# Attention scores made a second time transposed, with the maxima as extra rows, and values multiplied in float32 by four heads

## The chip, the cores and the metric

One core of one Trainium2 chip runs the whole program. The metric is device time in microseconds (us) of one execution, the median of several. The engines are TensorE (PE: matmuls and transposes; PEld is its weight load), VectorE (DVE), ScalarE (ACT), GpSimd (POOL) and SyncE (SP, which here only issues DMAs). Every engine runs its own program in order and waits on semaphores.

## The reference, cut to what matters

Two layers of an adaptive-layernorm model on X of 4 x 512 tokens x 256. Layer 0 is causal attention with 16 heads of 16, then a mixture of experts; layer 1 is a gated convolution, an MLP and another mixture of experts. The change is in layer 0's attention:

```
Q, K, V = heads(Xn @ Wq + bq), heads(Xn @ Wk + bk), heads(Xn @ Wv + bv)
scores  = where(causal, Q @ K.T / sqrt(16), -inf)      # 4 batches x 16 heads, 512 x 512
A       = softmax(scores, axis=-1)
out     = merge_heads(A @ V) @ Wo + bo
```

## The kernel before

The program is a row of blocks. The first block holds two stages, one behind the other on each engine: `attention_inputs` (modulation vectors, two layernorms, and Q, K, V of the four batches) and `attention`. The next block is `attention_output_and_dispatch` (output projection, residual, routing). A float32 value that has to keep its accuracy in a float32r matmul is split into a rounded part "hi" and a rest "lo", and a product is two or three matmuls.

**Inputs.** The work on the four batches is a wavefront: `wavefront` calls stages with lags, and the order of the calls is the order on the engine. PE makes Q, K and V, ACT and POOL make the hi and lo parts, SP stores them to DRAM (`q_parts`, `k_parts`, `v_parts`). POOL's order matters: `root(1)` (L267), the root that the second layernorm waits for, comes behind `zero` (lag 4), which clears the K4 and V4 buffers with four memsets (L574, L575). SP's order (L233 to L242) is store(0), store(1), the loads of quads 0 and 1, store(2), the keys of quad 2, store(3); then `attention` goes on with its own loads.

**Attention.** A quad is four heads of a batch; there are 16 quads, 64 heads. The loop is written for eight heads, run by a hardware loop, with heads at different stages beside one another. For a head, in order:
- PE, `scores` (L688, L689): for each query tile i of 128, one matmul of 128(i+1) keys over 128 rows (the parts of Q against those of K, other heads' rows zero), and one bf16 matmul that adds the causal mask.
- DVE, `maximum` (L786): the row's maximum, negated. ACT, `exponential` (L746): exp(score + that bias) into PR, with the sum of the row by the accumulator. DVE, the reciprocal (L812). POOL (L663): PR times the reciprocal.
- PE, `transposes` (L701): the ten 128x128 tiles of PR on and below the diagonal. ACT, `hi` (L756), copies them out of PSUM rounded, DVE, `lo` (L794), makes the rests.
- PE, `values` (L717): eight matmuls, V4 (128 columns, other heads' zero) by the hi and lo parts, 128 to 512 wide, four heads summed into one PSUM bank; ACT and DVE (L764, L816) split it into OT.

SP loads the next quad's K4 and Q4 when its scores have been read, and V4 likewise (L583 to L592). In the next block `products` (L1216) multiplies OT by Wo: for each batch and each of 2 halves, 4 quads x 3 matmuls of 512.

Of the kernel before, what the change touches and what calls it, by code (L numbers as in the profile page):

```python
# [7 lines left out]
F32 = mybir.dt.float32  # L8
# [54 lines left out]
def wavefront(*stages):  # L63

    for step in range(B + max(lag for lag, _ in stages)):
        for lag, stage in stages:
            if 0 <= step - lag < B:
                stage(step - lag)
# [14 lines left out]
class Core:  # L83

    def __init__(self, nc, ctx):
# [14 lines left out]
        self.v_parts = dram("v_parts", [B, TT, P, HEADS, 2 * DH])  # L100
# [41 lines left out]
def attention_inputs(k, heads, x, cT, wmod, w, ln_gb, bqk, bv_row):  # L142
# [8 lines left out]
    with ExitStack() as c:  # L151
        whi = k.sb("whi", [P, 3, DM, D], F32R, c)
        wlo = k.sb("wlo", [P, 3, DM, D], F32R, c)
        qhi = k.sb("qhi", [P, 4, T], F32R, c)
        qlo = k.sb("qlo", [P, 4, T], F32R, c)
        vf = k.sb("vf", [P, TT, D], F32, c)
        hhi = k.sb("hhi", [P, 2, DM, T], F32R, c)
        hlo = k.sb("hlo", [P, 2, DM, T], F32R, c)
        vp = k.sb("vp", [P, TT, HEADS, 2, DH], F32R, c)
        wm = k.sb("wm", [P, 2, DM, 6 * D], F32, c)  # L160
        qf = k.sb("qf", [P, 4, T], F32, c)

        odd = wm[:].rearrange("p l m n -> p (l m n)").bitcast(F32R).rearrange("p (i n) -> p i n", i=3)
        qhi = qhi[:], odd[:, 0].rearrange("p (j t) -> p j t", j=4)
        qlo = qlo[:], odd[:, 1].rearrange("p (j t) -> p j t", j=4)
        vp = vp[:], odd[:, 2].rearrange("p (t h a d) -> p t h a d", t=TT, h=HEADS, a=2)

        row = k.sb("row", [B, len(ROW_SETS), 2 * D], F32, c)
        sgn = k.sb("sgn", [P, D], F32, c)
        mag = k.sb("mag", [P, D], F32, c)  # L170
# [4 lines left out]
        hf = k.sb("hf", [P, DM, T], F32, c)  # L175

# [18 lines left out]
        v_ready, vf_done, vhi_done, vlo_done = S("v_ready"), S("vf_done"), S("vhi_done"), S("vlo_done")  # L195
        q_out, v_out = heads.q_out, heads.v_out
# [4 lines left out]
        def sync(sp):  # L201
# [18 lines left out]
            def store(b):  # L220
                for j in range(4):

                    sp.wait_ge(q_done, (b * 4 + j + 1) * 2)
                    sp.wait_ge(qlo_done, b * 4 + j + 1)
                    dst = (k.q_parts, k.k_parts)[j // 2]
                    for part, tile in enumerate((qhi[b % 2], qlo[b % 2])):
                        sp.dma_start(dst[b, 2 * (j % 2):2 * (j % 2) + 2, :, part].rearrange("q s r t -> (q s) r t"),
                                     f32(tile[:, j, :])).then_inc(q_out[j][b % 2], 16)
                sp.wait_ge(vhi_done, (b + 1) * 2)
                sp.wait_ge(vlo_done, (b + 1) * 2)  # L230
                sp.dma_start(k.v_parts[b].rearrange("t p h d -> p t (h d)"),
                             f32(vp[b % 2].rearrange("p t h a d -> p t (h a d)"))).then_inc(v_out[b % 2], 16)
# [3 lines left out]
            sp.wait_ge(heads.zeroed, 4)  # L236
            heads.wait_stored(sp, 0)
            for u in range(2):
                heads.load_keys(sp, 0, u, u)
                heads.load_values(sp, 0, u, u)  # L240
            store(2)
            sp.wait_ge(heads.s_ready, 16)  # L242
            heads.load_keys(sp, 0, 2, 0)
            store(3)

        def gpsimd(pool):
# [23 lines left out]
            def zero(b):  # L270
                if b == 0:
                    heads.zero(pool)
# [14 lines left out]
            def values_lo(b):  # L287
                for g in range(2):
                    pool.wait_ge(vhi_done, b * 2 + g + 1)
                    for t in (2 * g, 2 * g + 1):  # L290
                        last = pool.tensor_tensor(vp[b % 2][:, t, :, 1, :], vf[:, t, :].rearrange("p (h d) -> p h d", d=DH),
                                                 f32(vp[b % 2][:, t, :, 0, :]), ALU.subtract)
                    last.then_inc(vlo_done, 1)
            wavefront((8, values_lo), (0, root(0)), (4, zero), (5, root(1)), (7, queries(0)), (7, queries(1)), (7, queries(2)), (7, queries(3)), (6, store_rows))

        def scalar(act):
# [57 lines left out]
            def values(b):  # L354
                if b >= 2:
                    act.wait_ge(v_out[b % 2], b // 2 * 16)
                for g in range(2):
                    act.wait_ge(vf_done, b * 2 + g + 1)
                    for t in (2 * g, 2 * g + 1):
                        last = act.activation(vp[b % 2][:, t, :, 0, :], vf[:, t, :].rearrange("p (h d) -> p h d", d=DH), ACT.Copy)  # L360
                    last.then_inc(vhi_done, 1)

            wavefront((2, columns), (3, queries(0)), (3, queries(1)), (3, queries(2)), (0, first_norm), (0, evict), (1, weights), (1, second_norm),
                      (3, queries(3)), (3, values))

            for i in range(1, len(ROW_SETS)):
                act.wait_ge(k.rows_out[i], 16)

        def vector(dve):
# [106 lines left out]
            def values(b):  # L476
                if b:
                    dve.wait_ge(vhi_done, b * 2)
                    dve.wait_ge(vlo_done, b * 2)
                for g in range(2):  # L480
                    dve.wait_ge(v_ready, b * 2 + g + 1)
                    dve.tensor_tensor(vf[:, 2 * g:2 * g + 2, :], k.PS[:, 6 + g, :].rearrange("p (t d) -> p t d", t=2),
                                      bv[:].unsqueeze(1).to_broadcast([P, 2, D]), ALU.add).then_inc(vf_done, 1)
# [65 lines left out]
PT_AT = (0, 4 * P, 8 * P, 7 * P)  # L549
PT_BANKS = ((0, 4 * P), (4 * P, 4 * P), (8 * P, 2 * P))  # L550

class Heads:

    def __init__(self, k, c):
        self.k = k
        k.identb, k.maskb = (k.sb(n, [P, P], BF16, c, "right") for n in ("identb", "maskb"))
        self.Q4 = [k.sb(f"Q4_{u}", [P, 2, T], F32R, c, "right") for u in range(2)]
        self.K4 = [k.sb(f"K4_{u}", [P, 4, T], F32R, c, "right") for u in range(2)]
        self.V4 = [k.sb(f"V4_{u}", [P, TT, 4, P], F32R, c, "right") for u in range(2)]
        self.zeroed, self.s_ready = k.sem("zeroed"), k.sem("a2_s_ready")  # L560
        self.k_in, self.q_in, self.v_in = ([k.sem(f"{n}_in{u}") for u in range(2)] for n in "kqv")

        self.q_out, self.v_out = [[k.sem(f"q_out{j}{o}") for o in range(2)] for j in range(4)], [k.sem(f"v_out{o}") for o in range(2)]

    def wait_stored(self, eng, b):

        for odd in range(min(b + 1, 2)):
            for j in range(4):
                eng.wait_ge(self.q_out[j][odd], ((b - odd) // 2 + 1) * 32)
            eng.wait_ge(self.v_out[odd], ((b - odd) // 2 + 1) * 16)  # L570

    def zero(self, pool):
        for u in range(2):
            pool.memset(f32(self.K4[u][:]), 0.0).then_inc(self.zeroed, 1)  # L574
            pool.memset(f32(self.V4[u][:]), 0.0).then_inc(self.zeroed, 1)  # L575

    def load_keys(self, sp, b, q, u, halves=range(2)):

        for j in halves:
            r, heads = 64 * j, slice(j, 4, 2)  # L580
            src = self.k.k_parts[b, q, heads].rearrange("s a r t -> (a r) s t")
            for dup in range(2):
                sp.dma_start(f32(self.K4[u][r + 32 * dup:r + 32 * dup + 32, heads, :]), src).then_inc(self.k_in[u], 16)  # L583
            src = self.k.q_parts[b, q, heads]
            sp.dma_start(f32(self.Q4[u][r:r + 32]), src.rearrange("s a r t -> (a r) s t")).then_inc(self.q_in[u], 16)
            for dup in range(2):
                sp.dma_start(f32(self.Q4[u][r + 32 + 16 * dup:r + 48 + 16 * dup]),
                             src[:, 1 - dup].rearrange("s r t -> r s t")).then_inc(self.q_in[u], 16)

    def load_values(self, sp, b, q, u):  # L590
        for s in range(4):
            sp.dma_start(f32(self.V4[u][:, :, s, 32 * s:32 * s + 32]),  # L592
                         self.k.v_parts[b].rearrange("t p h d -> p t h d")[:, :, q * 4 + s, :]).then_inc(self.v_in[u], 16)

class OutputWeights:

    def __init__(self, k, c):
        self.st, self.w_in = k.sb("wo_st", [P, QUADS, D], F32, c), k.sem("wo_in")

    def load(self, sp, wo):  # L600
        for dup in range(2):
            for h in range(4):
                sp.dma_start(self.st[32 * h + 16 * dup:32 * h + 16 * dup + 16],
                             wo.rearrange("(q h r) n -> h r q n", q=QUADS, h=4)[h]).then_inc(self.w_in, 16)

def attention(k, inputs, heads, OT, out_weights, wo):

    nc = k.nc
    NQ = B * QUADS
    with ExitStack() as c:  # L610
        Q4, K4, V4, k_in, q_in, v_in = heads.Q4, heads.K4, heads.V4, heads.k_in, heads.q_in, heads.v_in
        k.sb("stored_last", [P, 5184], F32, c)
        PR = k.sb("PR", [P, 4, TT, T], F32, c)
        PThi = k.sb("PThi", [P, 2, 10 * P], F32R, c)
        PTlo = k.sb("PTlo", [P, 2, 10 * P], F32R, c)
        nmax = k.sb("nmax", [P, 4, TT], F32, c)
        rsum = k.sb("rsum", [P, 4, TT], F32, c)
        rinv = k.sb("rinv", [P, 4, TT], F32, c)
        carry = k.sb("carry", [P, 8], F32, c)
        S = lambda n: k.sem("a2_" + n)  # L620
# [2106 lines left out]
```

## Time and profile before

| | |
|---|---|
| median of 3 runs (lowest to highest) | 1127.13 us (1124.58 to 1129.17) |
| profiled execution: span of the core | 1155.7 us |
| PE busy | 957.4 us, 83% |
| DVE busy | 746.7 us, 65% |
| ACT busy | 657.2 us, 57% |
| POOL busy | 458.8 us, 40% |
| granted TensorE clock, mean | 0.911 |

The profile comes from one execution of its own. Its span (first to last instruction) is that execution's time as far as it is shown; it is 28.6 us above the median of the timed runs. "Granted clock" is the share of 2.4 GHz that the chip let TensorE have. Shares over the whole span mix stages with different limits, so the rows below are taken by stage: inputs from 0 to about 95 us, attention from there to 344, the output block behind it.

### The profile page before, as it was taken

To read this page: it belongs to the slowest core of one execution; us is meant where nothing else is said; L and a number is where in the kernel's file an instruction comes from. 1 tells how busy PE (TensorE), PEld (TensorE's weight loads), DVE (VectorE), ACT (ScalarE), POOL (GpSimd) and SP (SyncE) were. 2 spreads that over 40 slices of the span, in tenths; PEclk is the share of its full clock that TensorE was granted. 3 is DMA by queue.
4 is the path that set the end of the run, shared out by engine and by line. 5 is a ranking of instruction groups with operands and counts; after the bars stand their busy time and mean duration, and the time that the engine had idled before them with its cause. 6 is when DMAs were issued, how large, how long until landed. Compare 5 with 4: busy or idle time off the path is not lost. (4 is left out here: it accounts for less than half of the span.)

```text
span 1155.7 us, 21305 instructions
## 1 busy us (share of the span) xinstructions
PE 957.4 (83%) x5505; PEld 801.8 (69%) x5505; DVE 746.7 (65%) x1932; ACT 657.2 (57%) x1705; POOL 458.8 (40%) x641
## 2 busy tenths in 40 slices
PE   6678799999978744687999994078989998999994
PEld 2466688888866633465899994056867777888883
DVE  4885799999974753338755552799746777444453
ACT  3568889999972333327766663367853334433331
POOL 3477556666640566501344443457620111200000
PEclk8788999999997766798999997589989998999997
DMA  7067844444404422307543434730032232102012
GB/s 250 13 210 178 216 108 91 91 91 92 91 8 138 154 75 91 133 14 253 188 129 121 130 121 151 257 116 1 12 104 70 87 108 76 47 28 65 28 56 87
DMA packets 109867, 123.53 MB, mean 107 GB/s; under 512 B 44192, under 2 KB 82848, under 8 KB 109656
## 3 DMA queue, kind: packets, MB, share of 16 engines
q1 hardware_dynamic: 101128, 99.19, 30.5%
q0 software_dynamic: 8656, 23.33, 5.5%
q8 instruction: 40, 0.66, 0.2%
q14 instruction: 43, 0.35, 0.1%
HBM read 77.87 MB, written 44.62 MB: 106 GB/s over the span
## 5 line engine op out<-in xcount | busy, mean ns | idle before, releaser
L746 ACT ACTIVATE PR<-PS,nmax 128x128 f32<-128x128 f32 (+3 forms) x256 | 135.6, 551 | 12.6 <-DVE nmax L786 11.2
L663 POOL TENSOR_SCALAR PR<-PR,rinv 128x128 f32<-128x128 f32 (+3 forms) x256 | 132.3, 536 | 0.0
L786 DVE TENSOR_REDUCE nmax<-PS 128x1 f32<-128x128 f32 (+3 forms) x256 | 113.7, 481 | 20.2 <-PE PS L689 14.8
L1384 POOL DMA_INDIRECT r_results<-r_y,r_to x79 | 76.0, 963 | 112.8 <-DVE r_to L1439 76.6
L794 DVE TENSOR_TENSOR PTlo<-PS,PThi 128x512 fp32r<-128x512 f32 (+1 forms) x192 | 103.1, 590 | 2.9 <-ACT PThi L756 2.9
L756 ACT ACTIVATE PThi<-PS 128x512 fp32r<-128x512 f32 (+1 forms) x192 | 96.7, 545 | 6.1 <-PE PS L701 6.0
L688 PE MATMUL PS<-K,Q 128*128 128x128 f32 (+3 forms) x256 | 83.4, 385 | 12.0 <-DMA Q<-q_parts 8.9
L701 PE MATMUL PS<-ident,PR 128*128 128x128 f32 x640 | 85.8, 279 | 3.2 <-DVE PTlo L794 2.6
L717 PE MATMUL PS<-PThi,V 128*128 128x512 f32 (+3 forms) x256 | 85.1, 345 | 1.0 <-DVE PTlo L794 0.5
L2511 DVE TENSOR_TENSOR H<-PS,H 128x256 f32<-128x256 f32 x72 | 30.6, 424 | 81.9 <-ACT H L2472 80.2
L2472 ACT ACTIVATE H<-PS 128x256 f32<-128x256 f32 x72 | 27.6, 385 | 97.2 <-PE PS L2631 96.1
L978 POOL DMA_INDIRECT r_sorted<-o_hrow,o_slots x64 | 64.8, 1012 | 36.4 <-issue 18.7
L717 PE MATMUL PS<-PTlo,V 128*128 128x512 f32 (+3 forms) x256 | 76.0, 323 | 0.0
L1428 DVE TENSOR_TENSOR r_xlo<-PS,r_xhi 128x256 fp32r<-128x256 f32 x79 | 33.4, 423 | 65.4 <-issue 60.2
L701 PEld LDWEIGHTS PS<-ident,PR 128*128 128x128 f32 x640 | 68.8, 142 | 8.8 <-DVE PTlo L794 5.0
L2453 POOL DMA_INDIRECT x_results<-mlp_st,x_to x18 | 17.4, 966 | 143.0 <-DVE x_to L2506 118.7
L1399 ACT ACTIVATE r_xhi<-PS 128x256 fp32r<-128x256 f32 x79 | 30.4, 385 | 55.4 <-PE PS L2631 52.1
L2629 PE MATMUL PS<-r_wlo,r_xhi 128*128 x158 | 59.1, 374 | 2.5 <-issue 2.4
L688 PEld LDWEIGHTS PS<-K,Q 128*128 128x128 f32 x256 | 50.7, 202 | 15.0 <-ACT PR L746 7.4
L689 PE MATMUL PS<-maskb,identb 128*128 128x128 bf16 x256 | 60.1, 235 | 0.0
L2629 PE MATMUL PS<-u_lo,m_hi 128*128 (+1 forms) x144 | 59.1, 411 | 0.3 <-DVE m_lo L2493 0.3
L746 ACT ACTIVATION_READ_ACCUMULATOR PR<-PS,nmax 128x1 f32 x256 | 58.2, 227 | 0.0
(393 smaller groups left out, 3099.5 us busy)
## 6 DMA issues: line engine op xcount, KB each, us to landing
r_xg<-r_sorted SPq DMA_DIRECT2D x79, 129.0 KB
r_wst<-in_routed SPq DMA_DIRECT2D x16, 608.0 KB
K<-k_parts SPq DMA_DIRECT2D x64, 128.0 KB
Q<-q_parts SPq DMA_DIRECT2D x32, 128.0 KB
Q<-q_parts SPq DMA_DIRECT2D x64, 64.0 KB
V<-v_parts SPq DMA_DIRECT2D x64, 64.0 KB, 2.4
mlp_st<-r_results SPq DMA_DIRECT2D x8, 512.0 KB, 7.2
c_yg<-r_results SPq DMA_DIRECT2D x8, 512.0 KB, 8.3
```

The source lines that it names most:

```text
L663: pool.tensor_scalar(PR[:, e % 4, i, 0:w], PR[:, e % 4, i, 0:w], rinv[:, e % 4, i:i + 1], 1.0, ALU.mult, ALU.mult).then_inc(norm_done, 1)
L688: pe.matmul(k.PS[:, i, 0:w], Q4[u][:, s // 2, P * i:P * i + P], K4[u][:, s, 0:w], start=True, stop=False)
L689: pe.matmul(k.PS[:, i, w - P:w], k.identb[:], k.maskb[:], start=False, stop=True).then_inc(s_ready, 1)
L701: ins = pe.transpose(k.PS[:, 4 + bank, at % 512:at % 512 + P], PR[:, (e - TRANS) % 4, i, P * j:P * j + P], k.ident[:])
L717: ins = pe.matmul(O[:, P * j:T], V4[u][:, j, s, :], pt[:, ge % 2, PT_AT[j]:PT_AT[j] + w], start=(s == 0 and j == 0 and part == 0), stop=(s ...
L746: act.activation(PR[:, e % 4, i, 0:w], k.PS[:, i, 0:w], ACT.Exp, bias=nmax[:, e % 4, i:i + 1], accum_out=rsum[:, e % 4, i:i + 1]).then_inc ...
L756: act.activation(PThi[:, e % 2, at:at + w], k.PS[:, 4 + n, 0:w], ACT.Copy).then_inc(hi_done, 1)
L786: dve.tensor_reduce(nmax[:, e % 4, i:i + 1], k.PS[:, i, 0:P * (i + 1)], AX_X, ALU.max, negate=True).then_inc(max_done, 1)
L794: dve.tensor_tensor(PTlo[:, (e - LO) % 2, at:at + w], k.PS[:, 4 + n, 0:w], f32(PThi[:, (e - LO) % 2, at:at + w]), ALU.subtract).then_inc(l ...
L978: pool.indirect_dma_start(out=d.sorted, out_offset=bass.IndirectOffsetOnAxis(ap=slots[:, b * TT + t, choice:choice + 1], axis=0), in_=hrow ...
L1384: pool.indirect_dma_start(out=d.results, out_offset=bass.IndirectOffsetOnAxis(ap=to[:, i % TO_LANES:i % TO_LANES + 1], axis=0), in_=y[:, i ...
L2629: pe.matmul(out, x_hi, w_lo, start=first, stop=False)
```

## The change

- Scores are made twice. First per pair of heads as before (two heads in two banks, over 96 rows of hi/lo parts instead of 128), only for the maxima: one reduction for both heads (`maximum`). The negated maxima, split in two parts, are transposed on PE (`shift_rows`), copied to SBUF by ACT (`shift_row`) and put by four small DMAs from SP into rows 96 to 99 of Q. K has ones and zeros in these rows, so that the second scores (`columns`), keys on partitions, come out with the maximum already subtracted. The mask is added there too.
- ACT's exponential writes the transposed probabilities straight into PT (float32). Gone are the 640 transposes, the hi and lo parts of PR, POOL's scaling and the accumulators.
- `values`: V (float32, 16 columns and 16 ones per head) by PT (float32), one matmul per head and key tile; the four heads of a quad write four strips of 32 partitions of one bank. The ones give the row sums. The result is copied, transposed back (`rows`), divided (`normalize`), and per batch transposed again (`attended`) and split into OT.
- 32 pairs as one unrolled wavefront in place of the hardware loop, with lags from 0 to 6. Keys and queries have three buffers; V stays in SBUF, so `v_parts` and its hi/lo parts, stores and loads are gone.
- `zero` becomes `fill`: one memset of V, six of K and six `affine_select`s, at the same place in POOL's order.
- OT holds 2 instead of 4 tiles a batch, Wo 2 instead of 4 (one DMA), `products` 2 x 3 matmuls.

```diff
-            def zero(b):
+            def fill(b):
                 if b == 0:
-                    heads.zero(pool)
+                    heads.fill(pool)
...
             store(0)
             store(1)
-            sp.wait_ge(heads.zeroed, 4)
+            sp.wait_ge(heads.filled, heads.FILLED)
             heads.wait_stored(sp, 0)
-            for u in range(2):
-                heads.load_keys(sp, 0, u, u)
-                heads.load_values(sp, 0, u, u)
+            for quad in range(2):
+                heads.load(sp, quad)
             store(2)
-            sp.wait_ge(heads.s_ready, 16)
-            heads.load_keys(sp, 0, 2, 0)
+            heads.load(sp, 2)
             store(3)
...
+    def fill(self, pool):
+        ones = slice(SHIFT, P)
+        pool.memset(self.V[:].rearrange("p b t h e -> p (b t h) e")[:, :, DH:2 * DH], 1.0).then_inc(self.filled, 1)
+        for u in range(KQ_LANES):
+            pool.memset(f32(self.K[u][:]), 0.0).then_inc(self.filled, 1)
+        pool.wait_ge(self.filled, KQ_LANES + 1)
+        for u in range(KQ_LANES):
+            pool.memset(f32(self.K[u][ones]), 1.0).then_inc(self.filled, 1)
+        pool.wait_ge(self.filled, 2 * KQ_LANES + 1)
+        for u in range(KQ_LANES):
+            for j in range(2):
+                own = self.K[u][ones, j:4:2, :]
+                pool.affine_select(out=own, in_=f32(own), compare_op=ALU.is_ge, fill=0.0,
+                                   base=-2 if j else 1, pattern=[[0, 2], [0, T]], channel_multiplier=1 if j else -1).then_inc(self.filled, 1)
+        pool.wait_ge(self.filled, self.FILLED)
...
+    def load(self, sp, n, halves=range(2)):
+        b, q, u = n // QUADS, n % QUADS, n % KQ_LANES
+        for j in halves:
+            r, heads = ROWS * j, slice(j, 4, 2)
+            keys, queries = self.k.k_parts[b, q, heads], self.k.q_parts[b, q, heads]
+            sp.dma_start(f32(self.K[u][r:r + 32, heads]), keys.rearrange("s a r t -> (a r) s t")).then_inc(self.kq_in[u], 16)
+            sp.dma_start(f32(self.K[u][r + 32:r + 48, heads]), keys[:, 0].rearrange("s r t -> r s t")).then_inc(self.kq_in[u], 16)
+            sp.dma_start(f32(self.Q[u][r:r + 16]), queries[:, 0].rearrange("s r t -> r s t")).then_inc(self.kq_in[u], 16)
+            sp.dma_start(f32(self.Q[u][r + 16:r + 48]), queries.rearrange("s a r t -> (a r) s t")).then_inc(self.kq_in[u], 16)
...
+            for x in range(PAIRS):
+                sp.wait_ge(m_copied, x + 1)
+                for t in range(TT):
+                    sp.dma_start(f32(Q[x // 2 % KQ_LANES][SHIFT:SHIFT + 4, x % 2, t * P:(t + 1) * P]), mrow[4 * t:4 * t + 4, x % 2, :]).then_inc(m_in[x % 2], 16)
+                n, half = x // 2 + 2, x % 2
+                if KQ_LANES <= n < PAIRS // 2:
+                    load(n, half)
...
+            def columns(v):
+                def stage(x):
+                    lane, p, unit = x // 2 % KQ_LANES, x % 2, len(KEY_UNITS) * x + v
+                    if v == 0:
+                        pe.wait_ge(m_in[x % 2], 64 * (x // 2 + 1))
+                    wait(pe, exp_done, unit - 1)
...
+            def values(half):
+                def stage(x):
...
+                    for s in range(4):
+                        last = pe.matmul(O[32 * s:32 * s + 32, P * n:T], V[:, q // QUADS, n, 4 * (q % QUADS) + s, :],
+                                         PT[:, q % 2, s, CHUNK_AT[n]:CHUNK_AT[n] + w], start=(n == 0), stop=(n == 2))
...
+            wavefront((0, scores(0)), (2, columns(0)), (5, quads(rows)), (2, columns(1)), (0, scores(1)), (4, values(0)), (2, columns(2)),
+                      (1, shift_rows), (0, scores(2)), (2, columns(3)), (4, values(1)), (6, batches(attended(0))), (2, columns(4)),
+                      (0, scores(3)), (6, batches(attended(1))), n=PAIRS)
...
+            wavefront((2, exponential(0)), (2, exponential(1)), (2, exponential(2)), (1, shift_row), (2, exponential(3)), (6, batches(high(0))),
+                      (4, quads(attended_row)), (2, exponential(4)), (6, batches(high(1))), n=PAIRS)
...
+            wavefront((0, maximum(0)), (5, quads(normalize)), (0, maximum(1)), (0, maximum(2)), (6, batches(low(0))), (0, maximum(3)), (0, split_shift),
+                      (6, batches(low(1))), n=PAIRS)
...
-                    for q in range(QUADS):
-                        last = split3(pe, k.PS[:, 4 + m, :], whi[:, q, m * P:(m + 1) * P], wlo[:, q, m * P:(m + 1) * P],
-                                      OT[0][:, b * QUADS + q, :], OT[1][:, b * QUADS + q, :], q == 0, q == QUADS - 1)
+                    for f in range(DM):
+                        last = split3(pe, k.PS[:, 4 + m, :], whi[:, f, m * P:(m + 1) * P], wlo[:, f, m * P:(m + 1) * P],
+                                      OT[0][:, b * DM + f, :], OT[1][:, b * DM + f, :], f == 0, f == DM - 1)
```

## Rows read from the trace of the kernel before

**Rows 1.** Engines by stretch (start:end us, length, busy, clock, DMA share, GB/s).
```profile
100.00:150.00 50.00, 41.50 (x279) 35.36 (x279) 38.19 (x91) 40.17 (x128) 26.63 (x60) 0.90 0.76 196
200.00:250.00 50.00, 49.30 (x363) 42.27 (x361) 48.17 (x116) 48.13 (x158) 30.65 (x70) 1.00 0.45 97
```
**Rows 2.** Timeline of ACT (start us, length us): output copies of two quads.
```profile
201.49 0.62 ACT L764 ACTIVATE OT<-PS 128x512 f32 x1
...
330.81 0.62 ACT L764 ACTIVATE OT<-PS 128x512 f32 x1
```
**Rows 3.** Groups by line and shape, 40 to 345 us (busy us, mean ns).
```profile
L701 PE MATMUL PS<-ident,PR 128*128 128x128 f32 x640 | 85.8, 279 | 3.2 <-DVE PTlo L794 2.6 <-POOL PR L663 0.6
L756 ACT ACTIVATE PThi<-PS 128x512 fp32r<-128x512 f32 x128 | 79.2, 619 | 6.1 <-PE PS L701 6.0
L756 ACT ACTIVATE PThi<-PS 128x256 fp32r<-128x256 f32 x64 | 25.4, 396 | 0.0
L786 DVE TENSOR_REDUCE nmax<-PS 128x1 f32<-128x512 f32 x64 | 42.5, 665 | 1.2 <-PE PS L689 1.2
L786 DVE TENSOR_REDUCE nmax<-PS 128x1 f32<-128x256 f32 x64 | 27.0, 423 | 0.5 <-PE PS L689 0.5
```
**Rows 4.** Timeline of PE in one head: scores with mask, values, transposes.
```profile
201.33 1.29 PE L701 MATMUL PS<-ident,PR 128*128 128x128 f32 x10
...
202.37 0.31 PE L688 MATMUL PS<-K,Q 128*128 128x128 f32 x1
...
202.56 0.36 PE L688 MATMUL PS<-K,Q 128*128 128x256 f32 x1
...
203.44 0.39 PE L717 MATMUL PS<-PTlo,V 128*128 128x512 f32 x1
203.67 0.34 PE L717 MATMUL PS<-PThi,V 128*128 128x384 f32 x1
```
**Rows 5.** Timeline of PE: float32 matmuls of 512, and the clock then.
```profile
11.89 1.02 PE L494 MATMUL PS<-wm,scT 128*4 128x512 f32 x2
...
12.32 1.02 PE L494 MATMUL PS<-wm,scT 128*4 128x512 f32 x2
...
18.73 8.12 PE L494 MATMUL PS<-wm,scT 128*4 128x512 f32 x12
...
11.20:14.40 3.20, 3.20 (x8) 0.52 (x6) 2.95 (x13) 0.00 (x0) 0.17 (x1) 1.00 1.09 385
```
**Rows 6.** Timeline of POOL and DVE at the start of the inputs.
```profile
1.72 0.29 POOL L254 TENSOR_SCALAR_AFFINE_SELECT ident<-ident 128x128 f32<-128x128 f32 x1 [0.25 <-POOL onesb L252]
...
26.56 1.80 POOL L574 MEMSET K<- 128x2048 f32 x1
...
33.58 1.00 POOL L267 TENSOR_TENSOR rs<-var,mhalf 128x4 f32<-128x4 f32 x1
...
34.62 0.16 DVE L437 SCALAR_TENSOR_TENSOR nb<-mv,rs 128x4 f32<-128x4 f32 x1 [3.40 <-POOL rs L267]
```
**Rows 7.** Timeline of SP's issues, and first and last scores on PE.
```profile
81.83 2.95 SPq L583 DMA_DIRECT2D K<-k_parts  x2
...
145.02 3.96 SPq L603 DMA_DIRECT2D wo_st<-in_wo  x8
...
L688 PE MATMUL PS<-K,Q x256: 297/390/794, 94.9 to 330.3; 128*128 128x128 f32 x64, 128*128 128x384 f32 x64
```
**Rows 8.** DMA issues (count, KB each, median us from issue to landing).
```profile
V<-v_parts SPq DMA_DIRECT2D x64, 64.0 KB, 2.4
...
cs<-in_cT SPq DMA_DIRECT2D x1, 8.0 KB, 1.8
```
**Rows 9.** Timeline: end of attention on DVE, first output products on PE.
```profile
343.02 0.69 DVE L816 TENSOR_TENSOR OT<-PS,OT 128x512 fp32r<-128x512 f32 x1 [2.25 <-ACT OT L764]
...
346.98 0.63 PE L55 MATMUL PS<-OT,o_wlo 128*128 128x512 f32 x1
347.40 0.63 PE L56 MATMUL PS<-OT,o_whi 128*128 128x512 f32 x1
```

More of the change, by code:

```diff
@@ L61, in wait, with wavefront @@
         eng.wait_ge(sem, n)
-def wavefront(*stages):
-    for step in range(B + max(lag for lag, _ in stages)):
+def wavefront(*stages, n=B):
+    for step in range(n + max(lag for lag, _ in stages)):
         for lag, stage in stages:
-            if 0 <= step - lag < B:
+            if 0 <= step - lag < n:
                 stage(step - lag)
@@ L285, in queries @@
                 return stage
[L287 to L294, printed above, removed]
+            wavefront((0, root(0)), (4, fill), (5, root(1)), (7, queries(0)), (7, queries(1)), (7, queries(2)), (7, queries(3)), (6, store_rows))
         def scalar(act):
@@ L352, in queries @@
                 return stage
[L354 to L361, printed above, removed]
             wavefront((2, columns), (3, queries(0)), (3, queries(1)), (3, queries(2)), (0, first_norm), (0, evict), (1, weights), (1, second_norm),
-                      (3, queries(3)), (3, values))
+                      (3, queries(3)))
             for i in range(1, len(ROW_SETS)):
                 act.wait_ge(k.rows_out[i], 16)
+            act.wait_ge(qlo_done, B * 4)
         def vector(dve):
@@ L628, in _, with batches @@
+        def batches(stage):
+            return lambda x: stage(x // (2 * QUADS)) if x % (2 * QUADS) == 2 * QUADS - 1 else None
         @block.sync
@@ new lines, in _, with scores @@
+            turns = []
+            def scores(u):
+                def stage(x):
+                    lane, p, i, unit = x // 2 % KQ_LANES, x % 2, S_ORDER[u], 4 * x + u
+                    if u == 0 and p == 0:
+                        pe.wait_ge(kq_in[lane], 128 * (x // 2 // KQ_LANES + 1))
+                    w = P * (i + 1)
+                    if unit >= 2:
+                        pe.wait_ge(max_done, unit - 1)
+                    for j in range(2):
+                        pe.matmul(S_BANK(u, j)[:, 0:w], Q[lane][0:SHIFT, p, P * i:P * i + P], K[lane][0:SHIFT, 2 * p + j, 0:w], start=True, stop=False)
+                    for j in range(2):
+                        last = pe.matmul(S_BANK(u, j)[:, w - P:w], k.identb[:], k.maskb[:], start=False, stop=True)
+                    last.then_inc(s_ready, 1)
+                return stage
@@ new lines, in wait_side, with shift_rows @@
+            def wait_side(kind, i):
+                if turns:
+                    before, n = turns[-1]
+                    pe.wait_ge({"shift": m_copied, "rows": a_done, "columns": aT_lo}[before], n + 1)
+                turns.append((kind, i))
+            def shift_rows(x):
+                pe.wait_ge(shift_done, x + 1)
+                wait_side("shift", x)
+                pe.transpose(SIDE[0:4 * TT, 0:P], f32(shift[:, x % 2].rearrange("p t j a -> p (t j a)")), k.ident[:]).then_inc(mT_ready, 1)
@@ new lines, in rows, with attended, stage @@
+            def rows(q):
+                pe.wait_ge(o_copied, q + 1)
+                wait_side("rows", q)
+                for t in range(TT):
+                    last = pe.transpose(side(t), osb[:, t * P:(t + 1) * P], k.ident[:])
+                last.then_inc(oT_ready, 1)
+            def attended(m):
+                def stage(b):
+                    pe.wait_ge(a_done, (b + 1) * QUADS)
+                    wait_side("columns", b * DM + m)
+                    for t in range(TT):
+                        last = pe.transpose(side(t), A[:, b % 2, t, m * P:(m + 1) * P], k.ident[:])
+                    last.then_inc(aT_ready, 1)
+                return stage
```

366 lines of the change are left out of this document (142 added, 224 removed).

## The prediction

> **What bounds the kernel now.** I first looked at the engines by stretch, to find the stages. In attention's steady part PE is busy 49.3 of 50 us, DVE and ACT 48 each, at a granted clock of 1.00, which is 2.4 GHz; no engine waits for another for long, all three are full [rows 1]. So the next view is the pace, not a wait: ACT's copies of a quad's output lie 129.32 us apart over nine quads, 14.37 us a quad, 7.19 for two heads [rows 2]. The groups by shape say what fills the engines, and what the change takes away: 640 transposes, copies of 0.62 and 0.40 us on ACT and their like on DVE [rows 3]. All this work stands between 94.9 us and the end at 343.71 [rows 7, 9]. Ahead of the steady part, between 100 and 150 us, PE is less busy and DMA moves 196 GB/s: the stores of the inputs and the loads of the first quads are in each other's way there [rows 1]. Last I read the start of the inputs, where a wait of DVE ends at POOL [rows 6], since the change lengthens what POOL does there.
>
> **The new step.** One pass of the new wavefront handles a pair of heads; there are 32. Its work would fit in less than 7.19 us on every engine. ACT: five exponentials of 512 at 0.62, the copy of the shift at 0.29 (0.40 less half of 0.62 - 0.40) and half an output copy make 3.7. DVE: a 256-wide maximum takes 0.42 and a 512-wide one 0.67, so 128 more cost 0.12; pair maxima of 256, 512, 768 and 1024 make 3.15, with split and division 3.9 [rows 3]. PE is worked out below. What sets the step is, I think, a chain that goes round once per pass: `columns(0)` is second in PE's order and waits for the shift rows of its pair; those begin at `shift_rows` in the middle of the pass before, and go PE, ACT, SP, four DMAs, back to PE. PE takes its program in order, so while it waits nothing behind `columns(0)` runs, the next `shift_rows` included. A pass therefore lasts T1 (PE from `columns(0)` to the end of `columns(2)`) plus Tm (from there to the landing), if the PE work that lies beside Tm is shorter.
>
> Tm. ACT does exponential(2) before the shift's copy: 0.62 + 0.29 [rows 3]. SP issues four DMAs; eight issues took 3.96 us, so the fourth starts 1.5 us after the first [rows 7]. An 8 KB DMA landed 1.8 us after its issue, 64 KB ones after 2.4 [rows 8]; I take 1.8, since these carry 2 KB. With 0.2 for semaphores Tm is 4.4 us. Bounds: 3.2, if issue and landing took half a microsecond less each and nothing stood before the copy, and 5.2 with landings of 2.4. Beside it PE has shift, scores(2), columns(3), values(1), columns(4), scores(3) and the next scores(0), 2.4 us without the values and under 4.0 with them: hidden.
>
> T1. Pitches come from the starts of neighbours at full clock: 512 columns 0.23, a 128-wide score with its mask 0.19, a transpose 0.13 [rows 4]. columns(0) and (1) 0.29 each, scores(1) 0.35, columns(2) 0.35, `rows` 0.52 every second pass, 0.2 until the last result is out (a 384-wide matmul lasts 0.34 [rows 4], its pitch is about 0.18): 1.74 us. To this come the float32 values, and they are the main unknown. The six float32 matmuls of 512 of one layer's modulation rows (3 sets x 2 parts) stand in the trace as twelve records, and such records begin 0.43 us apart at clock 1.00 [rows 5]: two halves, 0.86 us in all, four times the 0.23 of the float32r form. Ahead of columns(2) stand 512 or 384 columns for four heads, 448 in the mean, so 0.75 us per head. One after another that is 3.0; all four at the same time 0.85. I take the case between: the second half of a head has to follow the first in the same strip, and the next head's first half may start with it, which makes five half slots of 0.37, 1.87 us. No row shows strips, so both ends stay in the range. T1 is then 3.6 and a pass 8.0 us, against 7.19 now.
>
> The Trainium skill, "TensorE: Matmul & The Clock Gate", Part 3 (packing small matmuls), says that matmuls in different column strips run at the same time (three strips measured 2.38 times faster), and that matmuls start and end in program order. The trace of before has no such case; read without the halves, the rule gives the 0.85 above and is the second rival. Its page "TensorEngine Tiling (Array Packing)", Key Properties, speaks against the change: going to another tiling drains the engine. Two runs of values a pass, each entered and left, at 0.2 us of drain (an estimate by the tail above) would be up to 0.4 us inside T1, 13 us over 32 passes; the sum goes without it.
>
> **The start.** POOL. Four memsets of 2048 took 7.02 us and the root behind them ended DVE's wait of 3.40 us [rows 6], so what `fill` adds delays the whole input stage. V has 4096 elements: 3.5 us; three K buffers 5.25; their 32 lower rows again with ones 5.25, as time goes by elements of a partition in these rows; six selects of 1024 elements, between 0.9 each (memset pace) and 2.3 (0.29 for 128 [rows 6]), say 1.25: 7.5. Together 21.5, a delay of 14.5 us (3 if 32 partitions count a quarter, 21 at the upper paces). Taken back: V's stores with their waits before the first load, and the V work of ACT and POOL, about 3. The loads begin at 81.83 + 11.5, about 93 us [rows 7], and the first scores at 106 instead of 94.9.
>
> SP. Before the first shift DMA SP must issue three quad loads of 0.75 MB, store(2) and store(3) of 2.1 MB each (8 x 256 KB), and Wo. At 196 GB/s [rows 1] 6.4 MB last 32 us, to 125. The maxima of the first pair would be ready by 113. With 2 us of landing columns(0) of pair 0 begins at 127 (113 if the shift were not held up, 132 if the rate is an eighth lower). Before, the same queue cost little, because only loads waited behind the stores.
>
> **The end.** Thirty-one passes of 8.0 after 127 reach 375. Then the last pass's rest (4.4 with its exponentials), two passes of values alone (2 x 2.2), output copy, transposes, division and the two splits in turn (6 to 7): 16, so 391 instead of 343.71, +47. Behind it the output block has half the products. The first batch's lie on the path, 12 fewer at 0.42 [rows 9], -5, and half the split of Wo -1; later batches also wait for routing on DVE, so I count nothing there (up to -9 more). Sum +41 on 1155.7. The timed median is 0.975 of that span, so I scale: +40, 1167 us.
>
> **The rivals.**
> 1. The strips don't run beside one another; the change doesn't do what "side by side" says. T1 4.7, pass 9.1: 127 + 282 + 20 = 429, +85 - 6, about 1204. For it: nothing in the trace shows overlap of matmuls.
> 2. Four abreast: T1 2.6, pass 7.0, 127 + 217 + 14 = 358, +14 - 6, about 1135. For it: the strips share no columns of the array; against: the halves.
> 3. The other side: the shift returns while PE is still at work, and PE's own sum is the pass. With four abreast that is 5.2 us, with a Tm of 3.2 a pass is 5.8: 127 + 180 + 14 = 321, -23 - 6, about 1099; at 5.2 it is 1079. The point from which it decides is a pass of 6.7 us, which gives no change with the late start. For it: 640 transposes and all the lo parts are gone, and DVE and ACT fall to about half; against: four issues and one landing alone are 3.3 us.
>
> Clock: PE would wait 1 to 2 us a pass. At 41.5 of 50 busy the granted clock was 0.90 [rows 1]; a fall to 1.2 GHz would double T1 there, so three passes of the 32 at the lower level would be +11 us. This is in the upper range.
>
> **How the numbers follow.** Forecast 0.40, rival 1 0.20, rival 2 0.18, rival 3 0.22. About 0.5%, 5.6 us, is what a measurement of this kernel can tell from no change. Rival 2 lies just above that line and its spread of 20 us goes to all sides (0.05 faster, 0.07 same, 0.06 slower); one in a hundred of rival 3 and of the forecast is "same". Faster 0.27, same 0.08, slower 0.65. The forecast's own range is 1140 to 1190 (start 10 us earlier or 5 later, pass 7.4 to 8.5). For 8 in 10 the range takes in rival 1's centre and the near half of rival 3: 1093 to 1210.
>
> **What would show it.** Right: PE waits once a pass at columns(0), ended by the shift DMA, 1 us or more; starts of one pair's columns(0) 8 us apart; float32 values of 512 for four heads in about 2.1 us (1.0 if four abreast, 3.4 if none); POOL's selects and memsets to about 48 us with DVE waiting for the root until then; a wait of 10 us or more at pair 0. Wrong: a pass below 6.7 us with PE busy throughout, or a shift that lands within 3 us of its transposition.

## The result, and the profile after

The changed kernel takes 1171.69 us (median of 4 runs, 1170.40 to 1175.92), the kernel before 1126.39 (4 runs). The ratio is 1.041, 95% interval 1.038 to 1.043: slower by 45 us. The forecast was 1167, in a range of 1093 to 1210. The profiled execution has a span of 1168.7 us.

The kernel before was profiled a second time, because the prediction's execution had lain 28.6 us above the median. Here are two stretches behind attention, first of the execution that the prediction was read from, then of the second one (columns as in [rows 1]):

```profile
400.00:450.00 50.00, 27.66 (x124) 21.98 (x124) 23.90 (x78) 22.32 (x35) 34.37 (x34) 0.70 0.24 85
450.00:500.00 50.00, 28.43 (x112) 22.35 (x113) 16.98 (x60) 12.91 (x22) 21.70 (x23) 0.72 0.30 104
```
```profile
400.00:450.00 50.00, 35.67 (x154) 28.13 (x155) 32.61 (x126) 26.50 (x42) 38.51 (x40) 0.76 0.29 104
450.00:500.00 50.00, 39.52 (x175) 30.55 (x174) 22.62 (x37) 20.83 (x34) 17.91 (x20) 0.92 0.36 118
```

The first execution did 19 us less of PE work in these 100 us: the excess lay behind attention, not in it; what caused it there is not shown. In the second, ACT's output copies are again 14.37 us apart over nine quads, and attention ends at 345.37. So that one (span 1128.0) is what after is held against. The end of attention on DVE, before (second profile) and after:

```profile
344.68 0.69 DVE L816 TENSOR_TENSOR OT<-PS,OT 128x512 fp32r<-128x512 f32 x1 [2.26 <-ACT OT L764]
```
```profile
389.38 0.69 DVE L809 TENSOR_TENSOR OT<-PS,OT 128x512 fp32r<-128x512 f32 x1 [1.44 <-ACT OT L769]
```

Attention ends 44.7 us later, the program 40.7 us later (1168.7 - 1128.0): what lies behind attention is 4.0 us shorter, in line with the shorter output projection. That size is rough, for in the runs below this part takes 775 to 781 us. All of the loss is ahead of 390 us, in three places.

**The fill.** POOL after, and the DVE instruction that waits for it (start, length, in brackets the idle time before it and who ended it); [rows 6] are its rows of before.

```profile
27.11 3.50 POOL L555 MEMSET V<- 128x4096 f32 x1
30.55 5.31 POOL L557 MEMSET K<- 128x2048 f32 x3
35.93 5.29 POOL L560 MEMSET K<- 32x2048 f32 x3
41.29 6.06 POOL L566 TENSOR_SCALAR_AFFINE_SELECT K<-K 32x1024 fp32r<-32x1024 f32 x6
47.44 1.01 POOL L255 TENSOR_TENSOR rs<-var,mhalf 128x4 f32<-128x4 f32 x1
```
```profile
48.48 0.16 DVE L410 SCALAR_TENSOR_TENSOR nb<-mv,rs 128x4 f32<-128x4 f32 x1 [16.10 <-POOL rs L255]
```

DVE now waits 16.10 us for the root, not 3.40 [rows 6]; everything behind it is late, the first scores come at 105.92 instead of 94.9 [rows 7].

**The first shift.** ACT has copied the first pair's maxima at 112.62, but SP is still at its stores; its DMAs for the shift begin 11.3 us later, and PE's first `columns(0)` comes at 130.03 after 13.53 us of idleness. ACT, SP and PE:

```profile
112.35 0.27 ACT L764 ACTIVATE mrow<-PS 16x128 f32<-16x128 f32 x1 [6.48 <-PE PS L699]
```
```profile
122.74 1.17 SPq L590 DMA_DIRECT2D wo_st<-in_wo  x1
123.95 2.63 SPq L637 DMA_DIRECT2D Q<-mrow  x4
```
```profile
130.03 0.80 PE L677 MATMUL PS<-Q,K 100*128 100x512 f32 x1 [13.53 <-DMA Q<-mrow]
```

**The passes.** Where PE was full before ([rows 1], 49.3 of 50 at 1.00), it is now 42 of 50 busy, at a granted clock of 0.93. Almost all its waiting is for the shift DMAs: 50.6 us in 29 waits, 13.5 of it the one above.

```profile
150.00:200.00 50.00, 42.00 (x313) 25.15 (x312) 26.19 (x47) 21.25 (x41) 0.00 (x0) 0.93 0.19 52
200.00:250.00 50.00, 42.41 (x319) 25.07 (x318) 24.73 (x45) 22.61 (x44) 0.00 (x0) 0.93 0.19 55
```
```profile
PE PS L677 <- DMA Q<-mrow: 50.6, 29, 13.5
```

Two passes of PE, cut to their landmarks: `columns(0)` (L677, 512 wide, with a wait), the values (L712), `shift_rows` (L699). A pass is counted from the start of one `columns(0)` to that of the next.

```profile
199.41 0.50 PE L677 MATMUL PS<-Q,K 100*128 100x512 f32 x1 [1.43 <-DMA Q<-mrow]
...
200.63 0.85 PE L712 MATMUL PS<-PT,V 128*32 128x384 f32 x8
201.41 0.50 PE L677 MATMUL PS<-Q,K 100*128 100x384 f32 x2
201.75 0.28 PE L685 MATMUL PS<-identb,maskb 128*128 128x256 bf16 x1
201.87 0.27 PE L699 MATMUL PS<-ident,shift 128*16 128x128 f32 x1
201.90 0.60 PE L659 MATMUL PS<-K,Q 96*128 96x384 f32 x2
...
202.98 0.64 PE L712 MATMUL PS<-PT,V 128*32 128x256 f32 x8
203.54 0.51 PE L677 MATMUL PS<-Q,K 100*128 100x256 f32 x2
...
206.59 0.50 PE L677 MATMUL PS<-Q,K 100*128 100x512 f32 x1 [1.40 <-DMA Q<-mrow]
...
208.20 1.91 PE L712 MATMUL PS<-PT,V 128*32 128x512 f32 x8
210.04 0.80 PE L677 MATMUL PS<-Q,K 100*128 100x384 f32 x2
...
210.87 0.42 PE L699 MATMUL PS<-ident,shift 128*16 128x128 f32 x1
...
215.45 0.50 PE L677 MATMUL PS<-Q,K 100*128 100x512 f32 x1 [1.09 <-DMA Q<-mrow]
```

The first pass lasts 7.18 us: 2.46 from `columns(0)` to the shift (T1), then ACT's copy ends 0.94 after the shift's start, SP's four DMAs begin 0.64 us apart, and PE goes on 4.72 us after that start (Tm; 4.54 in most passes). The second lasts 8.86: Tm is 4.58, but T1 is 4.28, where other passes with the same work (`rows` included) have 3.06. The two passes by the clock, and a stretch in the second:

```profile
199.40:206.60 7.20, 5.79 (x47) 3.42 (x47) 3.53 (x7) 3.55 (x7) 0.00 (x0) 1.00 0.22 61
206.60:215.45 8.85, 7.76 (x51) 4.33 (x51) 3.85 (x9) 3.13 (x6) 0.00 (x0) 0.81 0.16 42
208.30:211.70 3.40, 3.40 (x14) 1.29 (x14) 0.43 (x2) 0.84 (x3) 0.00 (x0) 0.50 0.04 15
```

In the middle of it PE is granted 0.50, that is 1.2 GHz: the 512-wide values take 1.84 us from their start to that of `columns(2)`. A later pass at full clock has 1.00 for the same eight records (240.91 to 241.90, with the mask ahead of them):

```profile
240.69 0.29 PE L661 MATMUL PS<-maskb,identb 128*128 128x128 bf16 x2
240.91 1.07 PE L712 MATMUL PS<-PT,V 128*32 128x512 f32 x8
241.90 0.50 PE L677 MATMUL PS<-Q,K 100*128 100x384 f32 x2
```

Such falls come in about ten of the 31 passes. Regular passes are 7.0 and 7.6 in turn, the longer ones with `rows`. Once a batch two passes are longer still, because `rows`, `attended` and the shift share one PSUM bank (SIDE) and wait for it in turn; these are called the batches' turns below. The mean from 130.03 to 372.90 is 7.83.

### The profile page after: what moved, and what is told of

It is laid out like the page before. It is cut to its first block and busy times, and to the rows that moved or that the text cites. A ratio compares the mean times of both kernels' runs of the same rounds, so it can differ in the third digit from the quotient of the medians.

```text
span 1168.7 us, 18258 instructions
## 1 busy us (share of the span) xinstructions
PE 934.9 (80%) x5361; PEld 724.8 (62%) x5361; DVE 650.5 (56%) x1644; ACT 539.6 (46%) x1185; POOL 315.1 (27%) x314
## 5 line engine op out<-in xcount | busy, mean ns | idle before, releaser
L783 DVE TENSOR_REDUCE nmax<-PS 128x2 f32<-128x1024 f32 (+3 forms) x128 | 104.8, 822 | 123.3 <-PE PS L661 123.2
L757 ACT ACTIVATE PT<-PS 128x512 f32<-128x512 f32 x160 | 93.8, 597 | 153.1 <-PE PS L685 151.6
L677 PE MATMUL PS<-Q,K 100*128 100x512 f32 (+3 forms) x256 | 83.7, 400 | 50.6 <-DMA Q<-mrow 50.6
L677 PEld LDWEIGHTS PS<-Q,K 100*128 100x128 f32 x256 | 46.2, 213 | 92.9 <-DMA Q<-mrow 55.7
L659 PE MATMUL PS<-K,Q 96*128 96x512 f32 (+3 forms) x256 | 76.0, 387 | 3.8 <-DVE nmax L783 2.4
L971 POOL DMA_INDIRECT r_sorted<-o_hrow,o_slots x64 | 63.8, 997 | 28.6 <-issue 18.7
L2623 PE MATMUL PS<-u_hi,m_lo 128*128 (+1 forms) x144 | 57.2, 397 | 0.0
L2624 PE MATMUL PS<-u_hi,m_hi 128*128 (+1 forms) x144 | 57.2, 397 | 0.0
L712 PE MATMUL PS<-PT,V 128*32 128x256 f32 (+3 forms) x512 | 55.7, 516 | 0.0
L2622 PE MATMUL PS<-r_wlo,r_hhi 128*128 x158 | 51.1, 323 | 1.4 <-DVE r_hlo L1442 1.4
L2624 PE MATMUL PS<-r_whi,r_xhi 128*128 x158 | 51.7, 327 | 0.0
L2623 PE MATMUL PS<-r_whi,r_xlo 128*128 x158 | 51.7, 327 | 0.0
```

What stands on the lines that cost most here:

```text
L659: pe.matmul(S_BANK(u, j)[:, 0:w], Q[lane][0:SHIFT, p, P * i:P * i + P], K[lane][0:SHIFT, 2 * p + j, 0:w], start=True, stop=False)
L677: last = pe.matmul(ST_BANK(unit)[:, at:at + w], K[lane][r, 2 * p + j, P * n:P * n + P], Q[lane][r, p, P * n:T], start=(at == 0), stop=False)
L712: last = pe.matmul(O[32 * s:32 * s + 32, P * n:T], V[:, q // QUADS, n, 4 * (q % QUADS) + s, :], PT[:, q % 2, s, CHUNK_AT[n]:CHUNK_AT[n] + ...
L757: act.activation(out, src, ACT.Exp).then_inc(exp_done, 1)
L783: dve.tensor_reduce(nmax[:, x % 2, i], k.PS[:, 2 * (u % 2):2 * (u % 2) + 2, 0:P * (i + 1)], AX_X, ALU.max, negate=True).then_inc(max_done, 1)
L971: pool.indirect_dma_start(out=d.sorted, out_offset=bass.IndirectOffsetOnAxis(ap=slots[:, b * TT + t, choice:choice + 1], axis=0), in_=hrow ...
```

## The experiments

Theory: the 45 us are the fill ahead of the second norm's root, the shift DMAs behind SP's stores, and the round of the shift, in which PE waits 1.2 to 1.45 us a pass. Rivals: PE's work, with its float32 values, sets the pass; the clock has nothing to do with the waits; stores and loads take the start's gains back. All compare with 1171.69 after and 1126 before (1125.94 to 1126.39 in the three series).

**Before, once more** (no edit).

> The kernel before once more, for a second profile. Theory: the 28.6 us by which its first profiled execution was above the median lie behind attention, in the routing between 420 and 520 us, so attention ends again at 343 to 345 us, ACT's output copies are 14.37 us apart, and the span is 1125 to 1130. Rival: the loss lies inside attention; then the copies are closer than 14.2 us and attention ends below 340.

Measured: the excess lay behind attention, as shown above; this execution took 1129.69 us. The end of attention, 345.37, is 0.4 us above what was expected. The theory holds; attention's pace of 7.19 us a pair, on which the prediction stands, is the same.

**The fill moved.**

```diff
+            heads.fill_zero(pool)            # V's ones, K's zeros: behind the constants
...
-            wavefront((0, root(0)), (4, fill), (5, root(1)), ...
+            wavefront((0, root(0)), (5, root(1)), ..., (6, store_rows), (5, fill_rest))
...
-            sp.wait_ge(heads.filled, heads.FILLED)
+            sp.wait_ge(heads.filled, KQ_LANES + 1)
```

> POOL's zeros and V's ones are written at the start, where POOL is idle from 2.9 to 14.6 us, the ones and selects in three pieces behind the roots. Theory: the fill delays the whole input stage; root(1)(0) at 28 to 34 us instead of 47.4, first scores 13 to 18 us earlier, the end of attention at 372 to 378 instead of 390, time 1153 to 1159 against 1171.7. Rival: the start of attention is set by the stores and loads on SP's queue anyway, which need the same time; then the first shift DMA is less than 5 us earlier and the time above 1166.

Measured: 1152.73 us (4 runs, 1149.4 to 1161.6), ratio to before 1.024 (1.018 to 1.030): 19 us gained. The root comes at 28.25:

```profile
2.81 3.50 POOL L558 MEMSET V<- 128x4096 f32 x1
...
28.25 1.01 POOL L256 TENSOR_TENSOR rs<-var,mhalf 128x4 f32<-128x4 f32 x1 [1.34 <-DVE var L407]
```

The root is 19.2 us earlier, the first scores 15.7 (90.17) and the first `columns(0)` 15.2 (114.80): most of the delay had been passed on, and the stores do not absorb the gain. Of the 19.2, 5.3 are a delay that the kernel before had too, its root being at 33.58 [rows 6]. In the profiled execution attention ends at 378.50, 11.6 us earlier and half a microsecond outside what was expected, since its 31 passes take 3.7 us more than in the changed kernel. The rest of the 19 lies behind attention (774.8 us against 778.6) and in the spread of the runs. The theory holds.

**The order of a pass.**

```diff
-  PE:  (2, columns(0)), (5, quads(rows)), (2, columns(1)), (0, scores(1)), (4, values(0)), (2, columns(2)), (1, shift_rows), ...
+  PE:  (2, columns(0)), (2, columns(1)), (1, shift_rows), (0, scores(1)), (4, values(0)), (5, quads(rows)), (2, columns(2)), ...
-  ACT: (2, exponential(0)), (2, exponential(1)), (2, exponential(2)), (1, shift_row), ...
+  ACT: (2, exponential(0)), (1, shift_row), (2, exponential(1)), (2, exponential(2)), ...
-  DVE: (0, maximum(0)), (5, quads(normalize)), (0, maximum(1)), ...
+  DVE: (0, maximum(0)), (0, maximum(1)), (5, quads(normalize)), ...
```

> Only the order in a pass: PE's shift_rows directly behind columns(1), rows behind values(0), ACT's shift_row behind exponential(0), DVE's normalize behind maximum(1). Theory: the pass is the round of columns(0) to shift_rows to the landing; its first part falls from 2.5 to 3.1 us to about 1, so the round falls to 5.5, and PE's own work of about 6.4 us sets the pass: 6.4 to 6.7 instead of 7.83, PE's waits at columns(0) under 0.3 us, end of attention 350 to 356, time 1130 to 1137. Rival A: PE's work, float32 values above all, sets the pass already: pass 7.5 to 8, time 1165 to 1175. Rival B: the waits also cost clock, and with PE full the stretches at half the clock go too: pass 6.0 to 6.3, time 1118 to 1126.

Measured: 1108.04 us (4 runs, 1105.4 to 1111.2), ratio to before 0.983 (0.981 to 0.986). By the order alone 64 us are gone, more than any of the three had said. Passes are 5.5 and 5.9 in turn, 5.96 in the mean with the batches' turns, and attention ends at 330.06. PE by stretch, and its waits for the shift:

```profile
150.00:200.00 50.00, 50.00 (x423) 31.01 (x425) 33.29 (x62) 28.63 (x58) 0.00 (x0) 1.00 0.27 74
```
```profile
PE PS L677 <- DMA Q<-mrow: 13.7, 2, 13.1
```

T1 is 0.75, and Tm is 4.14 where PE does wait for the shift (the last pass), so the round is 4.9 and no longer the longest; PE is full, at 1.00, and its own work is the pass. From the first to the last `columns(0)` it is 184.8 us instead of 242.9. Of these 58 us the waits are 36.5 (37.1 less 0.6); the other 21.5 are PE's work, done faster. At full clock a pass of the changed kernel has 5.6 us of it, or 6.4 with `rows` (7.00 less a wait of 1.43, 7.60 less 1.22), 6.0 in the mean against 5.7 here. So some 8 of the 21.5 come with the order itself, and about 13 are left for the clock, as many as the filler run below finds. My 6.4 fits only the passes with `rows`, and left the clock out: that is why the expectation was short. Rival A falls; B had the direction.

**No DMA for the shift.**

```diff
-                        pe.wait_ge(m_in[x % 2], 64 * (x // 2 + 1))      # in columns(0)
+                        pe.wait_ge(m_copied, x + 1)
...
-                pe.transpose(SIDE[0:4 * TT, 0:P], f32(shift[:, x % 2]...), k.ident[:])
+                for t in range(TT):
+                    last = pe.matmul(SIDE[SHIFT:SHIFT + 4, t * P:(t + 1) * P], f32(shift[:, x % 2, t]...), k.ident[:], ...)
...
-                act.activation(mrow[:, x % 2, :], SIDE[0:4 * TT, 0:P], ACT.Copy).then_inc(m_copied, 1)
+                act.activation(Q[lane][SHIFT:SHIFT + 4, x % 2, :], SIDE[SHIFT:SHIFT + 4, :], ACT.Copy).then_inc(m_copied, 1)
```

> No DMA for the shift: PE writes the four tiles of the shift to partitions 96 to 99 of the bank, four small matmuls for one, and ACT copies them from there into rows 96 to 99 of Q. The order of the stages is unchanged. Theory: from shift_rows to columns(0) is 2 us or less instead of 4.54, PE no longer waits at columns(0), the wait of 13.5 us at pair 0 behind SP's stores goes too; pass 6.5 to 6.8 with 0.3 for the three more matmuls, first columns(0) at 116 to 119, end of attention 338 to 346, time 1118 to 1130. Rival: PE's work sets the pass, only the start is gained: pass 7.6 to 8.1, time 1156 to 1163.

Measured: 1124.38 us (10 runs), ratio 0.998 (0.997 to 1.000). The time is as expected, PE does not wait at `columns(0)`, and the first one comes at 117.19. SP's four DMAs are gone. But the passes are 6.6 and 7.0 in turn, 6.94 in the mean with the batches' turns, not 6.5 to 6.8, for the new shift costs PE more than I had put down:

```profile
203.12 0.28 PE L681 MATMUL PS<-identb,maskb 128*128 128x256 bf16 x1
203.34 1.04 PE L696 MATMUL PS<-ident,shift 128*4 128x128 f32 x8
204.30 0.62 PE L655 MATMUL PS<-K,Q 96*128 96x384 f32 x2
```

Four small float32 matmuls take 0.96 us, start to start. From the start of the mask ahead of the shift to that of the scores behind it are 1.18 us (203.12 to 204.30), and in the changed kernel 0.15 (201.75 to 201.90): 1.03 us a pass more, not 0.3. This run is rid of the wait and of SP's queue, and is still 16 us behind the new order, which left the 13 us at the start.

**The first shifts from POOL.**

```diff
             inputs.gpsimd(pool)
+            for x in range(EARLY):          # EARLY = 2
+                put_shift(pool, x)          # the same four DMAs; SP begins with pair 2
...
```

> The shift DMAs of the first two pairs are issued by POOL, which has nothing left to do by then, instead of by SP behind its stores; all else as in the changed kernel. Theory: the first columns(0) need not wait for SP until 124 us; the first shift is copied at 112.6, issue and landing take 4 to 7 us beside the stores, so columns(0) of pair 0 comes at 117 to 120 instead of 130.0, the end of attention 9 to 13 us earlier, time 1158 to 1163. Rival: the stores keep the transfers busy, the landing of the first shifts or the loads of quad 3 behind the stores takes the gain back: time above 1167.

Measured: 1163.05 us (4 runs, 1160.8 to 1168.1), ratio 1.031 (1.028 to 1.035). The medians say 8.6 us, but the profiled execution, the slowest of the four, shows only 2.6 at the end of attention (387.52), where 9 to 13 were expected. The first two pairs' `columns(0)`:

```profile
119.62 0.79 PE L687 MATMUL PS<-Q,K 100*128 100x512 f32 x1 [2.75 <-DMA Q<-mrow]
...
130.04 0.79 PE L687 MATMUL PS<-Q,K 100*128 100x512 f32 x1 [2.99 <-DMA Q<-mrow]
```

Pair 0 is 10.4 us earlier; pair 1 still lands late, beside the stores, and 7.4 of it are left at pair 1 (130.04 instead of 137.40). By the last pass 2.7 are left; the other passes are 0.15 us longer in the mean, at a granted clock of 0.91 instead of 0.93 between 150 and 350 us. So the queue matters, but how much of the 13.5 it owns, 3 or 9 us, these runs leave open.

**One strip for all.**

```diff
-   last = pe.matmul(O[32 * s:32 * s + 32, P * n:T], V[...], PT[...], start=(n == 0), stop=(n == 2))
+   last = pe.matmul(O[0:32, P * n:T], V[...], PT[...], start=(n == 0 and s == 0), stop=(n == 2 and s == 3))
```

> All four heads' values go to the first 32 partitions of the bank, one after another; the other heads' rows of the output are left out. The work on TensorE is the same in columns, only the strips are not used side by side. Theory (four abreast in the changed kernel): a run of four with 512 columns takes 3.4 us instead of 0.85, values before columns(2) 2.2 us more in the mean, so the pass is 5.0 plus 4.5, 9.3 to 9.6 us instead of 7.83, attention ends at 435 to 445, time 1212 to 1232. Rival (the strips give nothing, or only two run abreast): the pass grows by less than 1.2 us, time below 1205.

Measured: 1229.9 us (one run), in the expected range. Regular passes are 8.9 and 10.2 in turn, 9.5 in the mean as expected, 9.67 with the turns of the batches; attention ends at 452.9, 8 us above the range that I had; from the last `columns(0)` to the end it takes 5.7 us more than the changed kernel. The values of 256 columns and what follows them:

```profile
200.04 1.91 PE L712 MATMUL PS<-PT,V 128*32 128x256 f32 x8
201.89 0.51 PE L677 MATMUL PS<-Q,K 100*128 100x256 f32 x2
```

1.85 us from start to start, against 0.56 (202.98 to 203.54) in the changed kernel: a factor of 3.3. Four strips do run at the same time.

**Useless work in the wait.**

```diff
+                    wait(pe, exp_done, unit - 1)
                     if v == 0:
+                        for _ in range(4):
+                            pe.matmul(ST_BANK(unit), K[lane][0:SHIFT, 2 * p, 0:P], Q[lane][0:SHIFT, p, :], start=True, stop=True)
                         pe.wait_ge(m_in[x % 2], 64 * (x // 2 + 1))
-                    wait(pe, exp_done, unit - 1)
```

The wait for ACT, which must have read the bank, moves ahead of the four.

> Four matmuls of 512 columns without use are put ahead of PE's wait at columns(0), into the bank that columns(0) then overwrites; nothing else is changed, the round of the shift is as long as before. They take 0.9 to 1.0 us and fit the wait of 1.2 to 1.45. Theory (a share of the loss is clock that PE's waits cost): granted clock 1.00 between 150 and 350 us instead of 0.93, passes of 7.0 and 7.6 throughout, mean 7.3, end of attention 14 to 18 us earlier, time 1153 to 1159. Rival: the falls of the clock don't come from these waits; the passes stay at 7.8 or grow, time 1168 to 1180.

Measured: 1158.86 us (4 runs, 1157.8 to 1163.7), ratio 1.029 (1.026 to 1.033): more work, 12.8 us less time. The clock, and the waits:

```profile
200.00:250.00 50.00, 46.00 (x346) 28.83 (x344) 26.79 (x50) 22.64 (x45) 0.00 (x0) 1.00 0.21 58
```
```profile
PE PS L679 <- DMA Q<-mrow: 26.2, 28, 12.5
```

The waits behind the first are down from 37.1 to 13.7 us, the granted clock is 1.00, and the regular passes are 7.0 and 7.6 throughout; with the batches' turns the mean is 7.42. From the first to the last `columns(0)` it is 229.9 us instead of 242.9, and attention ends at 376.52, 13.6 us earlier, just short of the 14 to 18 expected. The theory holds: PE's waits at `columns(0)` cost clock as well, some 13 us.

**Order, fill and first shifts together.**

> The new order of a pass, the fill spread as in e1, and the first two pairs' shift DMAs issued by POOL, together. Theory: three causes at three places, so the gains add: 63.6 by the order, 19 by the fill, 8 to 12 by the first shift: first columns(0) at 100 to 106, pass 5.9, end of attention 300 to 308, time 1076 to 1086. Rival: with the fill gone the stores of batches 2 and 3 come into the first passes, the loads of quads 2 and 3 are late, and PE waits for them: time 1088 to 1096.

Measured: 1082.33 us (5 runs, 1081.9 to 1085.4), ratio to before 0.961 (0.959 to 0.964). It beats both kernels, 44 us under the one before and 89 under the changed one; the three gains by themselves add to 91. First `columns(0)`, PE by stretch, end of attention:

```profile
103.56 0.77 PE L696 MATMUL PS<-Q,K 100*128 100x512 f32 x1 [3.17 <-DMA Q<-mrow]
```
```profile
200.00:250.00 50.00, 49.02 (x412) 30.22 (x411) 33.55 (x63) 28.61 (x57) 0.00 (x0) 1.00 0.26 74
```
```profile
301.96 0.69 DVE L828 TENSOR_TENSOR OT<-PS,OT 128x512 fp32r<-128x512 f32 x1 [1.44 <-ACT OT L788]
```

The pass is 5.97 us in the mean against 7.19 for the same two heads before: the new scheme itself is the faster one, once its chain is out of the way.

## Why the prediction was right, and where it was not

The sign, the cause and the number came out: slower, because a pass is a round through a DMA and not PE's work. But that the number is so close is luck: two wrong sizes cancelled.

| step | predicted | measured |
|---|---|---|
| root delayed by the fill | 14.5 us | 13.9 (47.44 against 33.58 [rows 6]) |
| first loads, first scores | 93, 106 | 89.8, 105.9 |
| first `columns(0)` | 127 | 130.0 |
| Tm | 4.4 | 4.54 |
| T1 | 3.6 | 2.76 at full clock (2.46 and 3.06) |
| pass, mean | 8.0 | 7.83 |
| end of attention | 391 | 390.1 |
| output block | -6 | -4.0 |

- **The step that failed is the float32 values, "five half slots of 0.37, 1.87 us".** I let only two heads run abreast, as no row showed strips. The rows after show 0.78 us for 384 columns (200.63 to 201.41) and 1.00 for 512 (240.91 to 241.90), all four heads, 0.89 in the mean, and the run in one strip shows the price without strips. So rival 2 was right in its mechanism, and with it the Trainium skill, "TensorE: Matmul & The Clock Gate", Part 3, that matmuls in different column strips run at the same time: this trace agrees, 1.85 us against 0.56. That step alone was 31 x 0.98 = 30 us too much. The rest of T1, 1.87 us instead of 1.74, gives 4 of them back, so T1 was 26 us too long in all.
- **What made up for it.** Mainly the clock. I had it only in the upper range, three passes, 11 us; it belonged in the centre: the regular passes alone would make 31 x 7.3 = 226 us, the trace has 243. The filler run gives about 13 of these 17 to the clock; the batches' turns took the other 4. The first `columns(0)` added 3.0 (SP came free at 123.95, near the 125 of the sum, but from its first issue to PE it took 6.1 us, not 2) and Tm 4.3. These are 24 of the 26; the end's last steps, 17.2 us instead of 16, the rest. Rival 2's own time, 1135, missed the same things.
- **The round of the shift** was right in mechanism and size. In Tm the parts were off in both directions: SP's issues 0.64 us apart, not 0.5, the last issue 1.66 before `columns(0)` instead of 2.0 with the 0.2 for semaphores, a term for which no row was given. The run in the new order shows it as the cause: the same instructions, the shift earlier, 64 us less. The run without the DMA agrees: no wait, 47 us less.
- **Rival 3**, PE's own sum as the pass, did not hold for the changed kernel; the new order makes it true. I had put PE's own sum at 5.2 us and, with a Tm of 3.2, the pass at 5.8; it is 5.5 and 5.9, and the time 1108 against 1079 and 1099. Tm did not fall to 3.2: the order took T1 down instead.
- **Rival 1**, no strips, was wrong; the run that makes it true gives 1230 against the 1204 written for it. Of the 26 us between, 18 are the passes, 9.67 against 9.1: T1 is 5.0, not 4.7, Tm 4.54, and the batches' turns come on top.
- **The drain** that the Trainium skill names in "TensorEngine Tiling (Array Packing)", Key Properties, was left out of the sum. The trace is in line with a small one: a run of values begins 0.22 us after the mask ahead of it (240.69 to 240.91) where scores begin 0.10 after theirs (204.25 to 204.35), and 512 columns take 1.00 against twice 0.43 [rows 5]. That would be about 0.26 us a run; no experiment took it apart from the loading of weights.
- **The base.** I scaled by the ratio of the median to the profiled span, as though that execution were evenly slow. It was not; the second profile shows attention untouched. The error was 1 us here.

## What to carry to other kernels

Where a value leaves an engine and comes back to it by other engines and a DMA, write the round down as a sum and start it as early in the pass as its inputs allow: here the order alone was worth 64 us, and the DMA need not go. A wait of an engine with a throttled clock can have a second price beside its length, here about 13 us beside 37; useless work in the gap, one small run, measures it. Constants belong where an engine is idle, not ahead of the step that others wait for: here that was worth 19 us.

## What the runs showed of the hardware

- The four heads' float32 matmuls leave eight records: four start within 0.021 us of one another and the other four 0.45 us later, again together (512 columns, single records at 240.9 us in the changed kernel). Read as first and second halves, they are in order within a strip and side by side across strips; the four heads together take 1.00 us, twice 0.43 being the time of one [rows 5].
- PE's granted clock between 150 and 300 us was 1.00 without waits for the shift (new order, no DMA), with a wait of 0.8 us in every second pass (one strip), and with four useless matmuls in each wait; with 1.2 to 1.45 us idle in most passes it was 0.92, in falls to 0.50 that each covered only part of a pass.
- POOL's memset takes the same time for 32 partitions as for 128 (5.29 and 5.31 us for three of 2048 elements), and an affine select of 1024 elements 1.01 us, not the 2.3 that 0.29 us for 128 would give.
